# Keeping the residual stream centred through four layers, and what that moves in the scan stage

## The chip, the cores and the metric

The kernel runs on one core of a Trainium2 chip. A core has a matrix engine (TensorE, PE here), a vector engine (VectorE, DVE), a scalar engine for functions and copies (ScalarE, ACT), a general engine (GpSimd, POOL) and a queue that starts transfers (SyncE, SP); they run their own instruction streams and wait for one another by semaphores. SBUF is the on-chip memory, PSUM the memory that PE writes its sums to. The metric is the time of one execution on the device in microseconds, lower is better.

## The reference

Four layers work on x of shape (2, 2048, 128), each with a layernorm ahead of it and one behind it, and a residual add:

```python
def _layernorm(x, axis=-1, eps=1e-05):
    m = jnp.mean(x, axis=axis, keepdims=True)
    v = jnp.var(x, axis=axis, keepdims=True)
    return (x - m) / jnp.sqrt(v + eps)
...
    x = x + _layernorm(_L0_attn_ref(_layernorm(x, axis=-1), ...), axis=-1)   # time mix
    x = x + _layernorm(_L0_ffn_ref(_layernorm(x, axis=-1), ...), axis=-1)    # gated feed-forward, ternary weights
    x = x + _layernorm(_L1_attn_ref(_layernorm(x, axis=-1), ...), axis=-1)   # state-space scan
    x = x + _layernorm(_L1_ffn_ref(_layernorm(x, axis=-1), ...), axis=-1)    # mixture of 8 experts, top 2
    return x
```

The third layer, for each token t, channel (256 of them) and state n (16):

```python
        proj = x @ W_in                                  # raw, gate
        conv = conv1d(raw, conv_w, 4 taps, causal)
        h = silu(conv + conv_b)
        ts, Bmat, C = split(h @ W_x); dt = softplus(ts @ W_dt + b_dt)
        dA = exp(dt * -exp(A_log)); dBu = dt * Bmat * h
        state = dA * state + dBu;  y = sum_n state * C
        y = (y + h * D) * silu(gate);  return y @ W_out
```

## The kernel before

The residual stream X lies in SBUF with the 128 channels on the partitions and the 2 x 2048 tokens along the row, in float32. It is worked on in eight tiles (t, b) of N = 512 tokens: b is the batch, t one of four pieces of the sequence. The four layers are four phases, each with its own program on every engine and a barrier between them: the time mix (0 to about 150 us of the profile), the feed-forward (to 470 us), the scan stage (to 975 us), the experts (to the end).

A layernorm over the partitions is done so: PE multiplies X by `G.centre` (the identity less 1/128 everywhere) into PSUM, which takes the mean off; ACT squares that; PE multiplies the squares by `G.ones` (1/128 everywhere), which gives the variance on every partition; ACT makes the inverse root of it with a logarithm and an exponential; DVE multiplies the centred tile by it.

In the scan stage each engine runs `body(t, b)` once per tile. There are eight such passes, counted 0 to 7 here, each with a loop over the 16 states n. For each state, ACT makes the decays (`decay`, two instructions, dA), PE spreads one row of B over the partitions into PSUM (`spread_B`, pD), ACT puts the tile's first value into column 0 of it (`splice`, one column), DVE multiplies that by dt times u (`dBu`, in place, pD<-dtu,pD) and runs the recurrence as one scan instruction (hs), POOL multiplies the result by C (`prod`), and PE adds the products over the states. dA, hs and prod are rings of a few buffers. Work for the next tile is written between the states by hand: `prep(t, b, step)` at the states that PE_PREP, ACT_PREP and the like list, and work for the tile before it (`tail`) at others. Ahead of the change the next tile's chain is: centre matmul (PE, n=0), square (ACT, n=0), variance matmul and root (PE and ACT, n=1), the copy of the last three columns of the previous xn to the front of the buffer (the halo of the convolution) and the multiply of xn (DVE, behind scan 1), convolution (PE, n=2 to 5), silus (ACT, n=6, which need another function table than the exponentials: one table load ahead, one behind), and so on to dt at n=12 and 13 on POOL. ACT also scales and rounds one expert weight (`split_weights`) in two places per pass in some passes.

At the end of the kernel the experts' outputs come back with tokens on the partitions, are normalised there, and PE turns each group of 512 tokens back with four transposes into PSUM (R1); DVE adds that to X, and SP stores X.

## Time and profile before

| | |
|---|---|
| median of 3 runs | 1278.0 us (1276.61 to 1281.53) |
| profiled execution | 1280.58 us, span 1278.8 us |
| PE busy | 1082.7 us (85%) |
| DVE busy | 955.2 us (75%) |
| ACT busy | 748.4 us (59%) |
| POOL busy | 730.6 us (57%) |
| granted clock of PE, mean | 0.946 of full speed |

The span is the time between the first and the last instruction that the profiler saw. The shares are means over four phases with different limits; they have to be read phase by phase. A busy time counts an instruction from its start to its end, with what it stands in between.

### The profile page before, as it was taken

The numbers are of one execution on the slowest core, as the hardware profiler recorded it, in microseconds if no ns is written. First come the engines' busy times: TensorE is split into PE (matmuls) and PEld (weight loads), VectorE is DVE, ScalarE is ACT, GpSimd is POOL, SyncE is SP. The second block draws the span as 40 slices with busy tenths as digits, with TensorE's granted clock in tenths as the row PEclk, the third lists the DMA queues.
The fourth block names the chain that finished last, engine by engine and source line by source line (L and its number), as shares of the span: only waits on it lengthen the run. The fifth ranks groups of instructions, "written<-read, shape, count | busy, mean of one in ns | idle before, by whom it ended". The sixth has DMA issues, their size and how long they took to land. (4 is left out here: it accounts for less than half of the span.)

```text
span 1278.8 us, 16507 instructions
## 1 busy us (share of the span) xinstructions
PE 1082.7 (85%) x4934; PEld 547.4 (43%) x4934; DVE 955.2 (75%) x1181; ACT 748.4 (59%) x1306; POOL 730.6 (57%) x640
## 2 busy tenths in 40 slices
PE   7876799999999987888989898989898388887853
PEld 3322244444444433333334333333335277776753
DVE  4898585665755439999999999999991876565545
ACT  6586545655556255767767686857653345454445
POOL 0222261431513005899898989897983167777764
PEclk8898899999999998999999999999998589999986
DMA  7000000000000003222322222222210111111225
GB/s 232 1 0 0 1 1 1 1 1 1 1 1 1 1 0 109 100 83 93 98 84 88 86 84 92 70 69 77 73 58 9 58 36 50 51 54 51 50 58 182
DMA packets 33966, 67.21 MB, mean 53 GB/s; under 512 B 7168, under 2 KB 7360, under 8 KB 33664
## 3 DMA queue, kind: packets, MB, share of 16 engines
q1 hardware_dynamic: 28464, 55.23, 13.4%
q0 software_dynamic: 4992, 10.23, 3.0%
q8 instruction: 42, 0.69, 0.2%
q10 hardware_dynamic: 432, 0.76, 0.2%
q14 instruction: 36, 0.29, 0.1%
HBM read 56.63 MB, written 9.57 MB: 52 GB/s over the span
## 5 line engine op out<-in xcount | busy, mean ns | idle before, releaser
L1936 POOL TENSOR_TENSOR prod<-hs,csb 128x1024 f32<-128x1024 f32 x128 | 301.9, 2359 | 125.3 <-DVE hs L1982 120.0
L1982 DVE TENSOR_TENSOR_SCAN hs<-dA,first,pD 128x1024 f32<-128x1024 f32 x128 | 300.4, 2347 | 5.2 <-DVE pD L1995 0.8
L1664 PE MATMUL pY<-prod,const 128*128 128x512 f32 x512 | 241.5, 597 | 5.0 <-POOL prod L1936 5.0
L1809 ACT ACTIVATE dA<-dt,negA 128x511 f32<-128x511 f32 x256 | 169.4, 712 | 1.5 <-DVE dt L2037 1.4
L1995 DVE TENSOR_TENSOR pD<-dtu,pD 128x1024 f32<-128x1024 f32 x128 | 154.9, 1211 | 10.0 <-ACT pD L1824 9.7
L1664 PEld LDWEIGHTS pY<-prod,const 128*128 128x128 f32 x512 | 97.5, 192 | 109.9 <-issue 92.2
L2471 POOL DMA_INDIRECT g<-moe_rows,source x78 | 82.4, 1056 | 55.5 <-DVE source L2666 26.7
L2717 DVE SCALAR_TENSOR_TENSOR hid<-pR,silu 128x512 f32<-128x512 f32 x78 | 53.9, 692 | 67.2 <-ACT silu L2425 67.2
L1162 ACT ACTIVATE stage<-pR,vec 128x512 f32<-128x512 f32 x64 | 43.9, 687 | 99.7 <-PE pR L891 99.5
L2490 POOL DMA_INDIRECT moe_outs<-y,to x78 | 81.1, 1039 | 26.2 <-issue 22.8
L1824 ACT ACTIVATE pD<-first 128x1 f32<-128x1 f32 x128 | 21.6, 169 | 119.4 <-PE pD L1674 98.2
L2425 ACT ACTIVATE silu<-pR 128x512 f32<-128x512 f32 x78 | 46.6, 597 | 73.9 <-PE pR L2210 73.9
L2208 PE MATMUL pR<-x,moe_hi 128*128 128x256 f16 x312 | 85.8, 275 | 1.2 <-DVE x L2701 1.2
L2210 PE MATMUL pR<-x,moe_lo 128*128 128x256 f16 x312 | 85.7, 275 | 0.0
L2209 PE MATMUL pR<-x,moe_hi 128*128 128x256 f16 x312 | 85.7, 275 | 0.0
L576 POOL TENSOR_TENSOR o<-o,rs 128x512 f32<-128x512 f32 x8 | 14.0, 1744 | 110.0 <-DVE o L692 110.0
L1674 PE MATMUL pD<-split,sel 96*128 96x512 bf16 x128 | 50.3, 393 | 28.4 <-DVE hs L1982 28.2
L1593 PE MATMUL pQ<-xn,convw 128*128 128x512 f32 x112 | 59.3, 656 | 15.0 <-DVE xn L1966 15.0
L1200 POOL TENSOR_TENSOR K_lo<-kstage,K_hi 128x512 f16<-128x512 f32 x24 | 29.1, 1217 | 52.0 <-DVE K_hi L1267 52.0
L1206 POOL TENSOR_TENSOR A_lo<-stage,A_hi 128x512 f16<-128x512 f32 x32 | 43.0, 1348 | 27.5 <-DVE A_hi L1341 27.5
L2320 PE MATMUL pY<-moe_hi,hid_hi 128*128 x312 | 56.4, 219 | 0.8 <-DVE hid_lo L2708 0.8
L2322 PE MATMUL pY<-moe_hi,hid_lo 128*128 x312 | 56.2, 219 | 0.0
(477 smaller groups left out, 2588.1 us busy)
## 6 DMA issues: line engine op xcount, KB each, us to landing
csb<-ssm_c SPq DMA_DIRECT2D x128, 256.0 KB, 3.1
raw<-moe_w SPq DMA_DIRECT2D x12, 512.0 KB, 4.8
room<-moe_outs SPq DMA_DIRECT2D x8, 512.0 KB, 8.3
hidw<-hid_w SPq DMA_DIRECT2D x1, 2048.0 KB, 10.0
moe_rows<-xt SPq DMA_DIRECT2D x8, 256.0 KB, 2.0
outT<-X SPq DMA_DIRECT2D x8, 256.0 KB, 2.0
X<-xT SPq DMA_DIRECT2D x3, 512.0 KB, 4.1
g<-moe_rows,source POOLq DMA_INDIRECT x78, 2.6
```

Source lines behind the costliest of these rows:

```text
L1593: last = nc.tensor.matmul(Q[c][:], convw[:, c, k, :], xn[b][:, k:k + N], start=k == 0, stop=k == TAPS - 1)
L1664: last = nc.tensor.matmul(YB[c][:], G.ident, prod[:, slot(b, n), c, :], start=n == 0, stop=n == DST - 1)
L1809: last = nc.scalar.activation(dA[:, slot(b, n), c, 1:N], dt[:, b, c, 1:N], ACT.Exp, scale=negA[:, c, n:n + 1])
L1936: nc.gpsimd.tensor_tensor(prod[:, slot(b, n), :, :], hs[:, slot(b, n), :, :], csb[:, slot(b, n), :, :].to_broadcast([P, CB, N]), ALU.mult)\
L1982: nc.vector.tensor_tensor_scan(hs[:, slot(b, n), :, :].rearrange("p c n -> p (c n)"), dA[:, slot(b, n), :, :].rearrange("p c n -> p (c n)" ...
L1995: nc.vector.tensor_tensor(both_dBu(n), dtu[:, b, :, :], bcastB(n).unsqueeze(1).to_broadcast([P, CB, N]), ALU.mult)\
L2208: nc.tensor.matmul(out, w_hi, x_hi, start=start, stop=False)
L2209: nc.tensor.matmul(out, w_hi, x_lo, start=False, stop=False)
L2210: return nc.tensor.matmul(out, w_lo, x_hi, start=False, stop=stop)
L2320: nc.tensor.matmul(out, hid_hi[:, n % HR, at], w_hi, start=u == 0 and h == 0 and r == 0, stop=False)
L2471: nc.gpsimd.indirect_dma_start(g[:, i % GR, r, :], None, rows, bass.IndirectOffsetOnAxis(ap=source[:, 2 * i + r:2 * i + r + 1], axis=0))\
L2490: nc.gpsimd.indirect_dma_start(outs, bass.IndirectOffsetOnAxis(ap=to[:, 2 * i + r:2 * i + r + 1], axis=0), y[:, i % YR, r, :], None).then_ ...
```

## The change

In phase 1 ACT copies each tile's centred value from PSUM back over X (`keep_centred`), and the matmuls that read X wait for that. The output of a layernorm has mean zero over the channels, so that X stays centred from then on: the centre matmuls of the later layernorms are taken out (two late in phase 1, six at the feed-forward's second half of the head, one at its end, seven in the scan stage and six in its last pass, two at the start of the experts), and squares and multiplies read X in SBUF instead of PSUM. The result needs the mean that was taken off: x is loaded again from memory (four tiles early in the last phase, four behind the experts' outputs), and a matmul by `G.ones` into the same PSUM as the transposes adds the mean, once per group.

In the scan stage a row's square no longer waits for PE, and stands on ACT at n=15 of the pass before the one that prepares it, with the three halo columns, which DVE no longer copies. Its variance and root are at n=0. PE does the spread of state 3 ahead of the convolution. ACT does the decays of states 7 and 8 ahead of the first table load, then the splice of state 7, the silus and the second load, then the splice of state 8. The weight splits are at n=1 and 3, and POOL's dt and dtu both at n=12.

```diff
                         pe.wait_ge(S["ln1"], at(t - 1, b))
+                        pe.wait_ge(S["x_centred"], at(t - 1, b))
                     if t >= 3:
...
                     nc.scalar.activation(rstd[:, b, :], lnv[:, b, :], ACT.Exp, scale=-0.5).then_inc(S["rstd"], 1)
+
+            def keep_centred(t):
+                for b in range(B):
+                    act.wait_ge(S["ln1"], at(t, b))
+                    nc.scalar.activation(X[:, b, ds(t)], C[b][:], ACT.Copy).then_inc(S["x_centred"], 1)
 
...
 
-            def next_square(b, ready, done):
+            def next_square(b, src, ready, done):
                 act.wait_ge(ready, b + 1)
-                nc.scalar.activation(hsq[:, b, :], V[b][:], ACT.Square).then_inc(done, 1)
+                nc.scalar.activation(hsq[:, b, :], src, ACT.Square).then_inc(done, 1)
 
...
             def next_square_B(b):
-                next_square(b, S["h_centredB"], S["h_squaredB"])
+                next_square(b, X[:, b, ds(FIRST)], S["h_addedA"], S["h_squaredB"])
 
...
             inverse_roots(0)
+            keep_centred(0)
             square(1)
...
                 log_of_sums(t)
+                if t + 1 < NT:
+                    keep_centred(t + 1)
                 if 1 <= t < NT - 1:
...
                 if g == 8:
-                    centre_B(t, 0)
                     values(t, 1)
...
                     variance_A(t, 1)
-                if g == 13:
-                    centre_B(t, 1)
                 if g == 14:
...
             pe.wait_ge(S["gelu2"], NT * B * FC)
-            nc.tensor.matmul(R[0][:], G.centre, X[:, 0, 0:N], start=True, stop=True).then_inc(G.ssm["centred"], 1)
             for c in range(CB):
...
             def square_B(t, b):
-                square(b, M[b], S["squaredB"], S["centredB"], ahead(t, b))
+                square(b, X[:, b, tile(t)], S["squaredB"], S["addedA"], ahead(t, b))
 
...
             def normalise_B(t, b):
-                scale(b, M[b], S["rstdB"], S["normedB"], ahead(t, b), z[:, b, :])
+                scale(b, X[:, b, tile(t)], S["rstdB"], S["normedB"], ahead(t, b), z[:, b, :])
 
...
                         accumulate(*before(t, b), DST - LAG + n)
+                    if n == 2:
+                        spread_B(t, b, n + 1)
                     if not is_last(t, b) and n in PE_PREP:
-                        prep(*after(t, b), PE_PREP.index(n))
-                    if n + 1 < DST:
+                        prep(*after(t, b), 1 + PE_PREP.index(n))
+                    if n != 2 and n + 1 < DST:
                         spread_B(t, b, n + 1)
...
 
-            PE_PREP, PE_TAIL, SKIP_AFTER = (0, 1, 2, 3, 4, 5, 6, 8, 9, 10), (12, 14), 7
+            PE_PREP, PE_TAIL, SKIP_AFTER = (0, 2, 3, 4, 5, 6, 8, 9, 10), (12, 14), 7
 
...
                 if step == 0:
-                    act.wait_ge(S["centred"], at(t, b))
-                    nc.scalar.activation(sq[:, b, :], Q[0][:], ACT.Square).then_inc(S["squared"], 1)
+                    wait_past(act, S["scaledC"], at(t, b) - 4)
+                    wait_past(act, S["split3"], at(t, b) - B)
+                    wait_past(act, S["c_out"], 16 * (at(t, b) - B))
+                    wait_past(act, S["b_out"], 16 * (at(t, b) - B))
+                    nc.scalar.activation(sq[:, b, :], X[:, b, ds(t)], ACT.Square).then_inc(S["squared"], 1)
+                    if not is_start(t):
+                        act.wait_ge(S["conv"], chunk(t, b, CB - 1) - B * CB)
+                        nc.scalar.activation(xn[b][:, 0:TAPS - 1], xn[b][:, N:N + TAPS - 1], ACT.Copy).then_inc(S["halo"], 1)
                 elif step == 1:
...
                 elif step == 4:
+                    act.preload_act_table_set("silu_and_others")
+                    splice(*before(t, b), 7)
                     act.wait_ge(S["parked"], chunk(t, b, CB - 1))
...
                         splice(t, b, 0)
-                    if n + 1 < DST:
+                    if n == 6:
+                        decay(t, b, 7)
+                        decay(t, b, 8)
+                        if is_last(t, b):
+                            splice(t, b, 7)
+                    elif n == 7:
+                        splice(t, b, 8)
+                    elif n + 1 < DST:
                         decay(t, b, n + 1)
...
                     if not is_last(t, b) and n in ACT_PREP:
-                        prep(*after(t, b), ACT_PREP.index(n))
+                        prep(*after(t, b), 1 + ACT_PREP.index(n))
                     if is_last(t, b) and n < 2 * EARLY:
...
                         tail(*before(t, b), ACT_TAIL.index(n))
-                    if splits(t) and n in (2, 7):
-                        split_weights(t, b, (2, 7).index(n))
+                    if splits(t) and n in (1, 3):
+                        split_weights(t, b, (1, 3).index(n))
+                    if splits(t) and n == 15:
+                        prep(t + 1, b, 0)
 
...
 
-            ACT_PREP, ACT_TAIL = (0, 1, 4, 5, 6, 8, 9, 10, 11, 12), (13, 14)
+            ACT_PREP, ACT_TAIL = (0, 4, 5, 6, 8, 9, 10, 11, 12), (13, 14)
             act.preload_act_table_set("natural_log_exp_and_others")
...
                     keep(t, b, n)
-                    if not is_last(t, b) and n in (8, 11, 12, 13):
-                        prep(*after(t, b), (8, 11, 12, 13).index(n))
+                    if not is_last(t, b) and n in (8, 11, 12):
+                        prep(*after(t, b), (8, 11, 12).index(n))
+                    if not is_last(t, b) and n == 12:
+                        prep(*after(t, b), 3)
                     if is_last(t, b) and n % 2 == 0 and 0 < n <= 2 * EARLY:
...
                 if not is_start(t):
-                    nc.vector.tensor_copy(xn[b][:, 0:TAPS - 1], xn[b][:, N:N + TAPS - 1]).then_inc(S["halo"], 1)
                     dve.wait_ge(S["halo"], at(t, b) - B)
-                nc.vector.tensor_tensor(xn[b][:, TAPS - 1:], Q[0][:], rstd[:, b, :], ALU.mult)\
+                nc.vector.tensor_tensor(xn[b][:, TAPS - 1:], X[:, b, ds(t)], rstd[:, b, :], ALU.mult)\
                   .then_inc(S["normed"], 1)
...
                 sp.dma_start(by_part[:, slab(i), :], xt[:, i % 2, :, :]).then_inc(S[f"rows_in{i % 2}"], 16)
+            def rows_again(i):
+                b, t = tile_of(i)
+                sp.dma_start(again[i], G.xT[:, b, t]).then_inc(S[f"x_again{i // (GROUPS // 2)}"], 16)
+
+            for i in range(GROUPS // 2):
+                rows_again(i)
             for r in range(YR):
...
                 sp.dma_start(back[:, :, slab(i), :], by_pair[:, :, slab(i), :]).then_inc(S[f"back{i}"], 16)
+            sp.wait_ge(S["down"], UNITS)
+            for i in range(GROUPS // 2, GROUPS):
+                rows_again(i)
             for i in range(GROUPS):
...
 
+            pe.wait_ge(S["silus"], UNITS)
             for i in range(GROUPS):
-                pe.wait_ge(S["scaledC"], i + 1)
                 if i >= 2:
                     pe.wait_ge(S["addedC"], i - 1)
+                pe.wait_ge(S[f"x_again{i // (GROUPS // 2)}"], 16 * (GROUPS // 2))
+                nc.tensor.matmul(R1[:, i % 2, :], G.ones, again[i], start=True, stop=False)
+                pe.wait_ge(S["scaledC"], i + 1)
                 for j in range(TC):
                     last = nc.tensor.matmul(R1[:, i % 2, j * P:(j + 1) * P], scaled[:, i % 2, j * P:(j + 1) * P], G.ident,
-                                            start=True, stop=True)
+                                            start=False, stop=j == TC - 1)
                 last.then_inc(S["turnedC"], 1)
...
             def square(i):
-                act.wait_ge(S["centred"], late(i) + 1)
-                nc.scalar.activation(sq[:, i % 2, :], R1[:, i % 2, :], ACT.Square).then_inc(S["squared"], 1)
+                b, t = tile_of(i)
+                nc.scalar.activation(sq[:, i % 2, :], X[:, b, t], ACT.Square).then_inc(S["squared"], 1)
 
```

On ACT in the scan stage, in a pass of the loop at states 6 to 8, this stood before. dA are the decays, pD<-first a splice, h and sgate the silus; the rows begin with the decays of state 7 and end with the splice of state 8.

```order
L1809 ACTIVATE dA<-dt,negA 128x511 x2
L1823 REGISTER_ALU
L1824 ACTIVATE pD<-first 128x1
L1740 ACT_TABLE_LOAD
L1740 ACTIVATE h_1<-h_1 128x1024
L1743 ACTIVATE sgate_1<-pQ_0 128x512
L1743 ACTIVATE sgate_1<-pQ_1 128x512
L1744 ACT_TABLE_LOAD
L1809 ACTIVATE dA<-dt,negA 128x511 x2
L1823 REGISTER_ALU
L1824 ACTIVATE pD<-first 128x1
```

It now reads:

```order
L1804 ACTIVATE dA<-dt,negA 128x511 x4
L1733 ACT_TABLE_LOAD
L1818 REGISTER_ALU
L1819 ACTIVATE pD<-first 128x1
L1736 ACTIVATE h_1<-h_1 128x1024
L1739 ACTIVATE sgate_1<-pQ_0 128x512
L1739 ACTIVATE sgate_1<-pQ_1 128x512
L1740 ACT_TABLE_LOAD
L1818 REGISTER_ALU
L1819 ACTIVATE pD<-first 128x1
```

Both pairs of decays (x4) stand ahead of the first table load, the splice of state 7 between that load and the silus, and behind the second load is only the splice of state 8.

On DVE in the scan stage, in a pass of the loop around scan 1 (hs is the scan, pD<-dtu,pD the multiply ahead of the next one, sq the inverse root), this stood before:

```order
L1995 TENSOR_TENSOR pD<-dtu,pD 128x1024
L1982 SCALAR_TENSOR_TENSOR hs<-dA,first,pD 128x1024
L1964 COPY xn<-xn 128x3
L1966 TENSOR_TENSOR xn<-pQ_0,sq 128x512
L1995 TENSOR_TENSOR pD<-dtu,pD 128x1024
L1982 SCALAR_TENSOR_TENSOR hs<-dA,first,pD 128x1024
```

It now reads:

```order
L2005 TENSOR_TENSOR pD<-dtu,pD 128x1024
L1992 SCALAR_TENSOR_TENSOR hs<-dA,first,pD 128x1024
L1976 TENSOR_TENSOR xn<-X,sq 128x512
L2005 TENSOR_TENSOR pD<-dtu,pD 128x1024
L1992 SCALAR_TENSOR_TENSOR hs<-dA,first,pD 128x1024
```

The copy of three columns is gone, and the multiply that makes xn reads X instead of PSUM.

On PE in the feed-forward, where the second centre matmul of a tile's head stands among those of another tile's layers (pR and pY are sums, hidw and cv are weights), this stood before:

```order
L890 MATMUL pR_2<-hidw,hid_hi 128x512
L891 MATMUL pR_2<-hidw,hid_lo 128x512
L928 MATMUL pM_0<-X,const 128x512
L889 MATMUL pY_1<-K_hi,cv_hi 128x512
L890 MATMUL pY_1<-K_lo,cv_hi 128x512
L891 MATMUL pY_1<-K_hi,cv_lo 128x512
```

It now reads:

```order
L894 MATMUL pR_2<-hidw,hid_hi 128x512
L895 MATMUL pR_2<-hidw,hid_lo 128x512
L893 MATMUL pY_1<-K_hi,cv_hi 128x512
L894 MATMUL pY_1<-K_lo,cv_hi 128x512
L895 MATMUL pY_1<-K_hi,cv_lo 128x512
```

The matmul of X by the constant is gone, and its neighbours follow one another.

## Rows read from the trace of the kernel before

**Rows 1.** Stretches: length; busy PE, PEld, DVE, ACT, POOL; clock, DMA share, GB/s.

```profile
150.00:470.00 320.00, 312.43 (x1302) 138.17 (x1302) 191.73 (x332) 170.66 (x231) 87.32 (x68) 0.99 0.00 1
486.00:960.00 474.00, 417.99 (x977) 168.60 (x978) 458.10 (x276) 330.06 (x618) 422.06 (x349) 0.97 0.27 83
```

**Rows 2.** Timeline of DVE, first and last scan: start, duration, operation.

```profile
486.81 2.35 DVE L1982 TENSOR_TENSOR_SCAN hs<-dA,first,pD 128x1024 f32<-128x1024 f32 x1
...
956.31 2.35 DVE L1982 TENSOR_TENSOR_SCAN hs<-dA,first,pD 128x1024 f32<-128x1024 f32 x1
```

**Rows 3.** Timeline of DVE, pass 5, scans 6 to 8.

```profile
807.49 2.35 DVE L1982 TENSOR_TENSOR_SCAN hs<-dA,first,pD 128x1024 f32<-128x1024 f32 x1
...
811.00 2.35 DVE L1982 TENSOR_TENSOR_SCAN hs<-dA,first,pD 128x1024 f32<-128x1024 f32 x1
814.88 1.23 DVE L1995 TENSOR_TENSOR pD<-dtu,pD 128x1024 f32<-128x1024 f32 x1 [1.53 <-ACT pD L1824]
816.14 2.35 DVE L1982 TENSOR_TENSOR_SCAN hs<-dA,first,pD 128x1024 f32<-128x1024 f32 x1
```

**Rows 4.** Waits of DVE, 480 to 960 us: total, times, longest.

```profile
DVE pD L1995 <- ACT pD L1824: 9.7, 13, 2.4
```

**Rows 5.** Timeline of ACT, pass 5, states 7 and 8.

```profile
805.70 1.32 ACT L1809 ACTIVATE dA<-dt,negA 128x511 f32<-128x511 f32 x2
808.63 0.17 ACT L1824 ACTIVATE pD<-first 128x1 f32<-128x1 f32 x1 [1.61 <-PE pD L1674]
808.82 1.28 ACT L1740 ACT_TABLE_LOAD   x1
810.11 1.06 ACT L1740 ACTIVATE h<-h 128x1024 f32<-128x1024 f32 x1
811.08 1.07 ACT L1743 ACTIVATE sgate<-pQ 128x512 f32<-128x512 f32 x2
812.16 1.28 ACT L1744 ACT_TABLE_LOAD   x1
813.45 1.33 ACT L1809 ACTIVATE dA<-dt,negA 128x511 f32<-128x511 f32 x2
```

**Rows 6.** Waits of ACT, 486 to 960 us: total, times, longest.

```profile
ACT pD L1824 <- POOL dtu L1910: 20.4, 7, 3.9
```

**Rows 7.** Groups of DVE instructions, 480 to 960 us: busy, mean ns, idle before.

```profile
L1966 DVE TENSOR_TENSOR xn<-pQ,sq 128x512 f32<-128x512 f32 x7 | 4.8, 688 | 0.2
L1964 DVE COPY xn<-xn 128x3 f32<-128x3 f32 x6 | 4.3, 718 | 0.0
```

**Rows 8.** Timeline of POOL and DVE around pass 5's halo copy.

```profile
788.63 2.36 POOL L1936 TENSOR_TENSOR prod<-hs,csb 128x1024 f32<-128x1024 f32 x1
...
789.93 1.09 DVE L1964 COPY xn<-xn 128x3 f32<-128x3 f32 x1
```

**Rows 9.** Timeline of POOL and DVE late in phase 1.

```profile
136.58 1.26 POOL L578 TENSOR_TENSOR XA<-o,xn 128x512 f32<-128x512 f32 x1
...
136.86 1.53 DVE L729 TENSOR_TENSOR X<-X,xn 128x512 f32<-128x512 f32 x1
```

**Rows 10.** PE's centring in phase 2: line L928, and the timeline at 453.80.

```profile
L928 PE MATMUL pM<-X,const x12: 592/592/593, 205.4 to 382.0; 128*128 128x512 f32 x12
...
453.80 1.02 PE L1037 MATMUL pR<-X,const 128*128 128x512 f32 x2
454.66 1.88 PE L1040 MATMUL pR<-stage,const 128*128 128x512 f32 x4
```

**Rows 11.** Timeline of the first microseconds: ACT, PE, DVE.

```profile
11.34 1.06 ACT L440 ACTIVATE rstd<-lnv 128x1024 f32<-128x1024 f32 x1
11.75 4.16 PE L256 MATMUL pC<-X,const 128*128 128x512 f32 x4 [2.57 <-DVE G L616]
...
20.60 1.28 DVE L625 TENSOR_TENSOR_SCAN run<-pK,run,bias 128x512 f32<-128x512 f32 x1 [6.82 <-PE pK L275]
```

**Rows 12.** Busy time by engine late in the last groups, columns as in rows 1.

```profile
1268.00:1270.00 2.00, 1.90 (x9) 1.61 (x9) 0.89 (x3) 0.03 (x1) 1.87 (x5) 0.50 0.34 130
```

More of the change, by code:

```diff
@@ L42 @@
     NV += _count
-SSM_NAMES = ("logA wsum wmean wcentred carry0 centred squared variance logs rstd normed halo conv parked projected gates "
+SSM_NAMES = ("logA wsum wmean wcentred carry0 squared variance logs rstd normed halo conv parked projected gates "
          "h xproj ts_in split1 whole rest1 split2 split3 dt_in magnitude expm log1p relu "
@@ L357, in next_variance_A @@
                 next_variance(b, S["h_squaredA"], S["h_varianceA"])
-            def next_centre_B(b):
-                pe.wait_ge(S["h_addedA"], b + 1)
-                nc.tensor.matmul(V[b][:], G.centre, X[:, b, ds(FIRST)], start=True, stop=True).then_inc(S["h_centredB"], 1)
             def next_variance_B(b):
@@ L733, in next_normalise @@
                 dve.wait_ge(S["h_rstdB"], b + 1)
[L734 removed]
+                nc.vector.scalar_tensor_tensor(out=hz[:, b, :], in0=X[:, b, ds(FIRST)], scalar=WS, in1=hsq[:, b, :],
                                                op0=ALU.mult, op1=ALU.mult).then_inc(S["h_normedB"], 1)
@@ L924, in variance_A @@
                 nc.tensor.matmul(Y[b][:], G.ones, sq[:, b, :], start=True, stop=True).then_inc(S["varianceA"], 1)
-            def centre_B(t, b):
-                pe.wait_ge(S["addedA"], ahead(t, b))
-                nc.tensor.matmul(M[b][:], G.centre, X[:, b, tile(t)], start=True, stop=True).then_inc(S["centredB"], 1)
             def variance_B(t, b):
@@ L1172, in _ @@
                 square_C(NT - 1, b)
-            act.wait_ge(G.ssm["centred"], 1)
-            nc.scalar.activation(z[:, 0, :], R[0][:], ACT.Square).then_inc(G.ssm["squared"], 1)
+            act.wait_ge(S["addedC"], at(P2_ORDER.index(0), 0))
+            nc.scalar.activation(z[:, 0, :], X[:, 0, 0:N], ACT.Square).then_inc(G.ssm["squared"], 1)
             act.wait_ge(G.ssm["variance"], 1)
@@ L1578, in prep @@
             def prep(t, b, step):
-                if step == 0:
+                if step == 1:
+                    pe.wait_ge(S["squared"], at(t, b))
                     wait_past(pe, S["relu"], chunk(t, b, 0) - 1)
-                    wait_past(pe, S["scaledC"], at(t, b) - 3)
-                    nc.tensor.matmul(Q[0][:], G.centre, X[:, b, ds(t)], start=True, stop=True)\
-                      .then_inc(S["centred"], 1)
-                elif step == 1:
-                    pe.wait_ge(S["squared"], at(t, b))
                     wait_past(pe, S["logC"], at(t, b) - 3)
@@ L1625, in next_stage @@
                     else:
-                        pe.wait_ge(S["next_parked"], i)
-                        pe.wait_ge(S["next_squared"], i)
-                    nc.tensor.matmul(Q[0][:], G.centre, X[:, i % B, (i // B) * N:(i // B + 1) * N], start=True, stop=True)\
-                      .then_inc(S["next_centred"], 1)
-                else:
-                    pe.wait_ge(S["next_squared"], i + 1)
-                    if i >= 1:
                         pe.wait_ge(S["next_logs"], i)
@@ L1637, in tail @@
             def tail(t, b, step):
-                if is_final(t):
-                    pe.wait_ge((S["next_parked"], S["next_logs"])[step], EARLY)
+                if is_final(t) and step == 1:
+                    pe.wait_ge(S["next_logs"], EARLY)
                 if step == 0:
@@ L2152, in phase_moe @@
         total = hid[:, :, :].rearrange("p r (j d) -> p r j d", j=TC)
+        again_0 = sb("again4", [P, GROUPS // 2, N])
+        spent = [w[:, :, :].rearrange("p r s -> p (r s)").bitcast(F32) for w in (hid_hi, hid_lo)]
+        again = [again_0[:, i, :] for i in range(GROUPS // 2)] + [w[:, k * N:(k + 1) * N] for w in spent for k in range(2)]
         sums = sb("sums4", [P, CHUNKS])
@@ L2210, in product @@
                 return nc.tensor.matmul(out, w_lo, x_hi, start=False, stop=stop)
-            def centre(i):
-                b, t = tile_of(i)
-                nc.tensor.matmul(R1[:, i % 2, :], G.centre, X[:, b, t], start=True, stop=True).then_inc(S["centred"], 1)
             def variance(i):
@@ L2241, in turn @@
                 last.then_inc(S["turned"], 1)
-            centre(EARLY)
-            centre(EARLY + 1)
             pe.wait_ge(S["consts"], 1)
```

44 lines of the change are left out of this document (24 added, 20 removed).

## The prediction

> **What bounds the kernel now.** I read the busy time by stage first. From 150 to 470 us PE is busy 312.43 of 320 us at a clock of 0.99: whatever leaves PE there shortens the run. From 486 to 960 us DVE is busy 458.10 of 474 us, PE 417.99 and POOL 422.06 [rows 1]; this is the scan stage. Its 128 scans start between 486.81 and 956.31 us, 469.5 us for 127 periods [rows 2]. An undisturbed period is 3.51 us (807.49 to 811.00): the scan and the next state's multiply, back to back. The next one in the same place took 5.14 us, since the multiply stood 1.53 us for ACT's splice [rows 3]. 127 periods of 3.51 are 445.8 us, so 23.7 us of the stage are something else, and the question for the change is what it does to these. The waits name the largest part: DVE waited 9.7 us in 13 stalls for splices [rows 4].
>
> **The scan stage: the splice of state 8.** Before the change ACT does, at n=6, the decays of state 7 (805.70), its splice (808.63, after a wait for PE), a table load, the silu, two gate silus, a second table load, and only then, at 813.45, the decays of state 8 and their splice [rows 5]. The multiply of state 8 could have gone at 814.88 - 1.53 = 813.35. In the new order both decay pairs stand ahead. With the durations of these rows: 805.70 + 1.33 + 1.33 = 808.36; table load 1.29 (start to start) to 809.65; splice 7, 0.17, to 809.82; silu 0.97 to 810.79; both gates 1.08 to 811.87; load 1.29 to 813.16; splice 8 to 813.33. That is 0.02 us ahead of 813.35: the stall goes, but with no reserve, and splice 7, now behind a table load, leaves at 809.82 instead of 808.80, which is about when multiply 7 wants it (scan 6 began at 807.49, so its multiply begins some 2.26 us later, 809.75). Rounding the pairs down to what fits in the stream gives some 0.2 us more. I therefore leave 0.8 us over the seven passes for a splice 7 or 8 that is still late.
>
> The other stalls in the 9.7 us are of states 0, 3 and 4. They stood behind ACT's two split copies of a weight (1.04 us each, moved from n=2 and n=7 to n=1 and n=3), behind the square and root of the next row (moved), and behind PE's convolution, which waited for xn ahead of state 3's spread (reordered), and POOL's dtu (moved ahead of one product). One of the 13, 0.3 us, is before the first scan and stays. So 9.4 us of waits can go, and each costs 5.14 - 3.51 - 1.53 = 0.10 us beside the wait: 12 x 0.10 = 1.2. The term is -9.4 - 1.2 + 0.8 = **-9.8 us**; its bounds are -11 (no stall left) and -5 (half of it remains because splice 8 is late by more than the rows say).
>
> The square and halo copy that ACT now does at n=15 come ahead of state 0's decays, some 0.7 us. They cost nothing as long as ACT waits there for POOL: it waited 20.4 us in seven times for POOL's dtu at exactly that splice, mean 2.9 us [rows 6]. POOL's dtu comes one product (2.36 us) earlier after the change, which leaves about 0.5 us of that cover, and DVE reaches the splice later than ACT. Without cover it would be 0.2 to 0.7 us per pass, up to 5 us in all.
>
> **The scan stage: xn.** DVE loses six halo copies, 4.3 us (mean 718 ns, for three columns), and keeps seven multiplies of 688 ns, 4.8 us [rows 7]. The gain of 4.3 us is what I doubt most. In pass 5 the copy lasted from 789.93 to 791.02, and POOL's product, which began at 788.63, ended at 790.99 [rows 8]: the copy itself is short, and it stood there until POOL's running instruction ended. The multiply behind it read one operand from PSUM and took its normal time. After the change it reads X and the root, both in SBUF. The only two-SBUF multiply or add of this shape next to a busy POOL is in phase 1: DVE's L729 began at 136.86 and took 1.53 us, ending 0.55 us after POOL's L578, which ended at 137.84 [rows 9]. So I take it that the new multiply waits as the copy did: up to 790.99 - 789.93 = 1.06 us in five of the seven passes (the copies' mean of 0.72 against 1.09 says that not every pass waits in full). That is -4.3 + 5.3 = **+1.0 us**. Bounds: -4.3 if it doesn't wait, +3.1 if it does in all seven passes.
> The Trainium skill, GPSIMD Engine Reference, section 1 (Specifications), says that the SBUF interfaces are shared with VectorE, with contention for DVE instructions in a 2-port mode or with two SBUF inputs. It speaks against this edit: the operand moved to SBUF puts the multiply under that rule. It gives no length; if the rule did not hold here, the scan stage would gain 5.3 us more, and the sum would be that of rival B.
> The other edits here change no engine that is waited for: PE loses a centre matmul per pass and six parks leave ACT in the last pass, where DVE had no wait.
>
> **Phase 2.** Six centre matmuls go, recorded as 12 halves of 592 ns. The pace in a full stream is seen at 453.80: a matmul of this form (two halves) starts, and the next starts at 454.66, 0.86 us later [rows 10]. With PE busy 98% of the stage, 6 x 0.86 = -5.2. The seventh, at 453.80 itself, stands ahead of the spread and the variance that open the scan stage: -0.86. ACT's squares lose a wait; DVE's six normalises read two SBUF operands, but DVE (191.73 of 320) and POOL (87.32) have room [rows 1]. The term is **-6.0**, bounds -6.5 and -3.5 (if DVE's work replaces PE as the last to arrive in some of the six places).
>
> **Phase 1.** The centre matmul of the second tile started at 11.75, before ACT's last inverse root was out at 11.34 + 1.06 = 12.40. It must now wait for an ACT copy of C, about 0.55 us (half of 1.07 for two gates from PSUM [rows 5]): 12.95, later by 1.2. DVE had no work but stood 6.82 us for PE at 20.60 [rows 11], so the delay goes through. The other copies lie in ACT's idle time, and the tail loses a matmul, some -0.3. Term **+0.9**, bounds +0.3 and +1.8.
>
> **Phase 4.** A centre pair leaves the start, -0.5. At the end eight matmuls of 128x512 enter PE ahead of each group's transposes. At full clock each is 0.86 us [rows 10] and fits while PE waits for POOL. But from 1268 to 1270 us, in the last groups, PE was busy 1.90 of 2.00 us at a granted clock of 0.50, which is 1.2 GHz [rows 12]; there each costs 1.7 and there is no room. I take +0.5, bounds -0.5 and +4. The reload of x is early for half the tiles and behind the read-back of the expert outputs for the rest, needed only at the fifth group. Term **0.0**.
>
> **Sum.** -9.8 + 1.0 - 6.0 + 0.9 + 0.0 = -13.9 us. The profiled execution took 1280.6 us (span 1278.8), 2.6 above the median of 1278.0; the difference carries over to the median unchanged: 1264.1, and I give **1264 us**.
>
> **Rivals.** A difference of about 0.5% (6.4 us) is what a measurement of this kernel can tell from none.
> B: xn does not wait for POOL. Then the scan stage gains 5.3 us more: 1259 us. For it: the one wait of phase 1 is of another POOL operation. Against: it ended with POOL's instruction. Chance 0.13.
> C: the reordered ACT still delivers splice 7 or 8 late, half the waits remain (+5), and POOL's dtu no longer covers the n=15 work: 1269 to 1272. For it: 0.02 us of reserve. Chance 0.15.
> D: the change does little: phase 2 only moves its wait to DVE (-3.5), the stalls move from state 8 to state 7 (-3), and the end pays 2 us: about 1275. Chance 0.09.
> E, slower: DVE's multiply does not get in at the end of POOL's instruction, but loses to POOL's queued ones. POOL nearly always has a product ready, 2.36 us each [rows 8]. One more per pass is 7 x 2.36 = 16.5 us, which cancels the 13.9 (break-even at 2.0 us per pass); slower by 6.4 from 2.9 us per pass, so with two products: 1264 + 33 = 1297. Against: the copy and L729 both got through at the end of the first instruction [rows 8, 9]. Chance 0.04.
> My own sum, 1260 to 1267, has 0.59.
>
> **Numbers.** The range is 1256 to 1270: it takes in B, my case with its bounds and most of C, and leaves out D, E and the far end of C. Faster by over 0.5% means below 1271.6: my case, B and nearly all of C, 0.84. Same: D and the rest of C, 0.11. Slower: E and an unseen one, 0.05.
>
> **What would show it.** In the scan stage: first to last scan 460 to 462 us instead of 469.5; no wait of a multiply for ACT above 0.4 us; xn's multiplies of 1.7 us in the later passes (of 0.69: B; of 4 and more: E). Phase 2 shorter by 6 us with PE still busy 98% of it; the second tile's centre matmul at 12.95. At the end: the ones matmuls inside PE's waits, and the distance from the first transpose to the last DVE add within 1 us of before. The prediction is wrong if splice 8 is still what DVE waits for, if the end runs at 1.2 GHz with PE as its bound, or if POOL holds the multiply for more than one instruction.

## The result and the profile after

The changed kernel takes 1271.07 us (median of 9 executions, 1269.25 to 1274.82) beside 1280.66 for the kernel before on the same chip (9 executions, 1276.61 to 1281.68): a ratio of 0.9933, interval 0.9919 to 0.9948. It is faster by 9.6 us, where 13.9 were forecast. The kernel before was itself 2.7 us slower in these nine executions than the 1278.0 that the forecast stood on; the rest of the distance to 1264, 4.4 us, is a wrong sum. Taken from 1280.66, the same sum would have given 1266.8 and its upper bound 1272.7. The measured time lies among rival C's 1269 to 1272, but not for C's reasons, as the states below show.

The page of the profiled execution of the changed kernel, its span and its row of granted clock:

```profile
span 1269.3 us, 16484 instructions
...
PEclk8898899999999998999999999999896599999897
```

The span is 9.5 us shorter. The first and the last scan (DVE's timeline of the changed kernel) divide it, as [rows 2] do for before:

```profile
480.74 2.35 DVE L1992 TENSOR_TENSOR_SCAN hs<-dA,first,pD 128x1024 f32<-128x1024 f32 x1
...
945.21 2.35 DVE L1992 TENSOR_TENSOR_SCAN hs<-dA,first,pD 128x1024 f32<-128x1024 f32 x1
```

| stretch, us | before | after | difference | forecast |
|---|---|---|---|---|
| start to first scan (phases 1 and 2) | 486.8 | 480.7 | -6.1 | -5.1 |
| first to last scan | 469.5 | 464.5 | -5.0 | -8.8 |
| last scan to the end | 322.5 | 324.1 | +1.6 | 0.0 |
| span | 1278.8 | 1269.3 | -9.5 | -13.9 |

Each number is of one profile, and of the kernel before there is only one. How far such numbers move shows in the profiles of the second run and the experiments below: with the changed kernel's code, start to first scan is 479.0 to 482.1 us (eleven profiles), first to last scan 462.0 to 464.8 (five), and last scan to the end 321.6 to 328.1 (seven). So the +1.6 is not told from none, and the -5.0 could have come out as -7.5.

In the scan stage every scan start is in the trace. The start-to-start time less 3.505 us (an undisturbed period), summed over the passes by the state that the period ends in, shows where DVE loses its time. Not all of it is waiting: some 3.6 us at state 0 and 4.2 at state 2 are multiplies of DVE's own that stand there, of 128x512 and 0.60 us each (for the tile before in six passes, xn in seven). "again" is the changed kernel in a second profile (below); the lines under it are experiments. States that are not shown hold under 0.6 us together. Three more profiles, of experiments that leave the scan stage as in the changed kernel, have 5.4 to 5.5 at state 1, 7.0 to 7.1 at state 2, and 464.6 to 464.8 in all.

| us lost at state | 0 | 1 | 2 | 3, 4 | 7 | 8 | 11, 12 | first to last scan |
|---|---|---|---|---|---|---|---|---|
| before | 5.2 | 0.3 | 8.8 | 2.1 | 0.0 | 7.9 | 0.0 | 469.5 |
| after | 3.9 | 6.4 | 6.1 | 0.0 | 1.4 | 0.0 | 1.3 | 464.5 |
| again | 3.9 | 5.3 | 6.1 | 0.0 | 0.4 | 0.0 | 1.1 | 462.0 |
| dtu behind product 13 | 5.0 | 0.3 | 7.6 | 0.1 | 1.4 | 0.0 | 1.3 | 461.2 |
| spread of state 1 first | 3.9 | 0.3 | 9.1 | 0.0 | 0.0 | 0.0 | 0.9 | 459.4 |
| root in PSUM | 3.9 | 6.8 | 4.2 | 0.2 | 1.0 | 0.0 | 1.1 | 462.6 |
| both of these | 3.9 | 0.3 | 5.2 | 0.2 | 1.0 | 0.0 | 1.1 | 457.1 |
| both, and PE busy at the barrier | 3.9 | 0.3 | 4.2 | 0.0 | 0.0 | 0.0 | 0.9 | 454.5 |
| old order of states 7 and 8 | 3.9 | 4.6 | 6.7 | 0.0 | 0.0 | 8.4 | 0.0 | 468.7 |

State 8's 7.9 us are gone, and so are those of states 3 and 4. In their place stands a loss at state 1 that was 0.3 us before and that no rival named. Behind the first pass no multiply of state 0 waits for ACT, so that what ACT now does at n=15 costs nothing. DVE's waits of the changed kernel, against [rows 4] of before:

```profile
DVE pD L2005 <- ACT pD L1819: 7.3, 8, 2.7
```

Eight waits instead of 13, of 7.3 us instead of 9.7. In pass 1, DVE's timeline of the changed kernel (scan 0, the multiply and the scan of state 1):

```profile
539.09 2.35 DVE L1992 TENSOR_TENSOR_SCAN hs<-dA,first,pD 128x1024 f32<-128x1024 f32 x1
544.11 1.23 DVE L2005 TENSOR_TENSOR pD<-dtu,pD 128x1024 f32<-128x1024 f32 x1 [2.67 <-ACT pD L1819]
545.38 2.35 DVE L1992 TENSOR_TENSOR_SCAN hs<-dA,first,pD 128x1024 f32<-128x1024 f32 x1
```

The multiply waits 2.67 us for ACT's splice, which waits for PE's spread. PE's timeline of the changed kernel at the same place:

```profile
537.95 3.78 PE L1650 MATMUL pY<-prod,const 128*128 128x512 f32 x4 [2.94 <-POOL prod L1945]
541.53 1.91 PE L1579 MATMUL pQ<-sq,const 128*128 128x512 f32 x2
543.24 0.63 PE L1660 MATMUL pD<-split,sel 96*128 96x512 bf16 x1
```

PE adds up product 13 of the old tile (537.95, after standing 2.94 us for POOL), then the next row's variance (541.53), and only then spreads B for state 1 (543.24). The product was late on POOL, whose timeline in the changed kernel shows why:

```profile
529.93 2.36 POOL L1891 TENSOR_TENSOR dt<-dt,dtu 128x1024 f32<-128x1024 f32 x1
532.36 2.36 POOL L1895 TENSOR_TENSOR dtu<-dt,h 128x1024 f32<-128x1024 f32 x1
...
535.54 2.36 POOL L1945 TENSOR_TENSOR prod<-hs,csb 128x1024 f32<-128x1024 f32 x1
```

dt and dtu stand one behind the other, and product 13 begins at 535.54, behind both. Before the change it stood between them, and PE added it up without a wait ahead of state 1's spread (timelines of POOL and PE in the kernel before, same pass):

```profile
537.97 2.34 POOL L1886 TENSOR_TENSOR dt<-dt,dtu 128x1024 f32<-128x1024 f32 x1
540.27 2.34 POOL L1936 TENSOR_TENSOR prod<-hs,csb 128x1024 f32<-128x1024 f32 x1
...
542.71 2.33 POOL L1890 TENSOR_TENSOR dtu<-dt,h 128x1024 f32<-128x1024 f32 x1
```

```profile
542.83 1.88 PE L1664 MATMUL pY<-prod,const 128*128 128x512 f32 x4
544.55 1.02 PE L1582 MATMUL pQ<-X,const 128*128 128x512 f32 x2
545.96 0.39 PE L1674 MATMUL pD<-split,sel 96*128 96x512 bf16 x1 [0.39 <-DVE hs L1982]
```

In the changed kernel PE stands 2.1 to 2.9 us for product 13 in each of the seven passes that have a tile before them; in the kernel before it does in none. In pass 1 the granted clock is 0.50, or 1.2 GHz, behind that idle time, and the sum of four matmuls takes 3.78 us, twice the 1.88 that it takes elsewhere in this trace at 1.00 (busy time by engine in the changed kernel; the clock is third from the right, ahead of the share of the transfer engines and GB/s):

```profile
532.00:535.00 3.00, 3.00 (x8) 1.04 (x6) 2.96 (x3) 2.34 (x6) 2.92 (x4) 1.00 0.06 23
...
538.00:541.00 3.00, 3.00 (x4) 1.45 (x5) 2.96 (x2) 0.00 (x0) 3.00 (x4) 0.50 0.25 87
```

The multiply of xn did wait for POOL as forecast, where it got that far. The group in the changed kernel, against [rows 7], and POOL's and DVE's timelines in pass 5:

```profile
L1976 DVE TENSOR_TENSOR xn<-X,sq 128x512 f32<-128x512 f32 x7 | 6.5, 932 | 0.0
```

```profile
780.31 2.35 POOL L1945 TENSOR_TENSOR prod<-hs,csb 128x1024 f32<-128x1024 f32 x1
782.61 0.66 POOL L1938 COPY carry<-hs 128x2 f32<-128x2 f32 x1
```

```profile
781.47 1.75 DVE L1976 TENSOR_TENSOR xn<-X,sq 128x512 f32<-128x512 f32 x1
...
804.18 1.21 DVE L2005 TENSOR_TENSOR pD<-dtu,pD 128x1024 f32<-128x1024 f32 x1
```

From 781.47 the multiply stood until POOL's product ended (780.31 + 2.35 = 782.66), and took 1.75 us; POOL's small copy behind it took 0.66 instead of 0.19. But in five of the seven passes it took 0.67 to 0.7: in four of these, DVE had been held in state 1, and POOL had used that time. Rivals B and E both fall: the multiply waits, and none takes more than 1.98 us in any profile of this study.

ACT's timeline in pass 5 of the changed kernel, against [rows 5]; the multiply of state 8 is the last row above:

```profile
795.26 2.54 ACT L1804 ACTIVATE dA<-dt,negA 128x511 f32<-128x511 f32 x4
797.82 1.28 ACT L1733 ACT_TABLE_LOAD   x1
799.12 0.17 ACT L1819 ACTIVATE pD<-first 128x1 f32<-128x1 f32 x1
...
801.26 1.28 ACT L1740 ACT_TABLE_LOAD   x1
802.55 0.17 ACT L1819 ACTIVATE pD<-first 128x1 f32<-128x1 f32 x1
```

Splice 8 was out at 802.72, and DVE wanted it at 804.18: 1.5 us of reserve, not 0.02, since ACT comes to decay 7 earlier against DVE than before (3.15 us ahead of the start of scan 6, where it was 1.79).

Behind the scan stage, the first and the last matmuls of PE's scores in the changed kernel, and its busy time around them:

```profile
966.33 3.58 PE L2246 MATMUL pX<-gatew,convw 128*128 128x8 f32 x16 [4.55 <-DVE later L2541]
...
989.24 1.06 PE L2257 MATMUL pY<-ident,g 128*128 128x128 f16 x8
```

```profile
963.00:966.00 3.00, 0.00 (x0) 0.00 (x0) 1.17 (x11) 1.73 (x2) 0.53 (x4) 0.61 0.04 8
966.00:978.00 12.00, 11.67 (x52) 9.70 (x53) 2.41 (x7) 4.59 (x9) 4.54 (x4) 0.50 0.06 22
978.00:990.00 12.00, 12.00 (x81) 11.54 (x79) 4.68 (x8) 6.67 (x12) 4.57 (x4) 0.50 0.29 110
```

and the same matmuls in the kernel before:

```profile
979.00:988.00 9.00, 9.00 (x48) 7.78 (x46) 0.69 (x1) 2.48 (x5) 2.72 (x3) 0.52 0.00 0
988.00:998.00 10.00, 9.07 (x81) 8.35 (x81) 5.11 (x9) 7.28 (x14) 5.72 (x5) 0.82 0.35 134
```

PE is idle 4.55 us ahead of the scores (2.6 us before, where the pair of centre matmuls stood in between), and the clock stays at 0.50 for all of the 24 us that the scores and their transposes take. In the kernel before it is 0.52 until 988 and 0.82 in the 10 us behind. The first gather of an expert's rows starts 69.6 us behind the last scan, and 67.3 before.

### The profile page after: what moved, and what is told of

Same layout as the page of the kernel before. It is cut to its first block and busy times, and to the rows that moved or that the text cites. A ratio compares the mean times of both kernels' runs of the same rounds, so it can differ in the third digit from the quotient of the medians.

```text
span 1269.3 us, 16484 instructions
## 1 busy us (share of the span) xinstructions
PE 1080.5 (85%) x4902; PEld 548.9 (43%) x4902; DVE 953.0 (75%) x1175; ACT 749.6 (59%) x1314; POOL 735.4 (58%) x640
## 3 DMA queue, kind: packets, MB, share of 16 engines
q1 hardware_dynamic: 29616, 57.33, 13.9%
## 5 line engine op out<-in xcount | busy, mean ns | idle before, releaser
L1650 PE MATMUL pY<-prod,const 128*128 128x512 f32 x512 | 247.6, 609 | 16.9 <-POOL prod L1945 16.9
L580 POOL TENSOR_TENSOR o<-o,rs 128x512 f32<-128x512 f32 x8 | 13.9, 1743 | 110.1 <-DVE o L696 110.1
L1586 PE MATMUL pQ<-xn,convw 128*128 128x512 f32 x112 | 56.6, 641 | 3.0 <-DVE xn L1976 3.0
```

What stands on the lines that cost most here:

```text
L1650: last = nc.tensor.matmul(YB[c][:], G.ident, prod[:, slot(b, n), c, :], start=n == 0, stop=n == DST - 1)
```

## The experiments

The first four (dtu, spread, root, both) ran on one chip, and the changed kernel, as far as is known, on others. Their whole times compare with it only by way of the kernel before on each chip; the losses by state are the firmer evidence.

**dtu behind product 13 again.** Edit:

```diff
-                    if not is_last(t, b) and n in (8, 11, 12):
-                        prep(*after(t, b), (8, 11, 12).index(n))
-                    if not is_last(t, b) and n == 12:
-                        prep(*after(t, b), 3)
+                    if not is_last(t, b) and n in (8, 11, 12, 13):
+                        prep(*after(t, b), (8, 11, 12, 13).index(n))
```

> The changed kernel with one part undone: POOL makes dtu behind product 13 again, as before the change. In the changed kernel DVE lost 6.4 us in state 1 (PE spreads B for state 1 only after it stood for POOL's product 13 at state 0). Theory W: that product is late because dtu stands ahead of it on POOL; then the state-1 loss falls below 1 us, state 0 rises from 3.9 to about 5, and first to last scan falls from 464.5. Rider P: POOL is nearly full, so that DVE, no longer held in state 1, waits for POOL's port at xn instead: state 2 rises from 6.1 to about 9 us, and the stage ends near 462. Rival V: it is the variance matmul, now ahead of that spread, that makes it late; then state 1 keeps about 6 us.

Measured: 1264.36 us, ratio to before 0.9882 (0.9860 to 0.9904). State 1 loses 0.3 us instead of 6.4, state 0 5.0, state 2 7.6; the stage takes 461.2 us. DVE's waits for splices in this kernel:

```profile
DVE pD L2003 <- ACT pD L1819: 1.9, 5, 0.9
```

W holds and V falls: the variance matmul stands where it stood, and the loss is gone. P holds in part at most: state 2 is 1.5 us above the first profile of the changed kernel, but 0.5 above three others. The profiled execution was the slowest of the five, 1271.25 us: the 3.3 us that its scan stage is shorter are lost again ahead of it and behind it.

**The spread of state 1 first.** Edit:

```diff
+                    if n == 0:
+                        spread_B(t, b, n + 1)
                     if n < LAG and not is_first(t, b):
                         accumulate(*before(t, b), DST - LAG + n)
...
-                    if n != 2 and n + 1 < DST:
+                    if n not in (0, 2) and n + 1 < DST:
```

> The changed kernel, with PE's spread of B for state 1 moved ahead of the sum of the old tile's product 13 and of the variance matmul. W and V both expect the state-1 loss of 6.4 us to fall below 0.5 us. Rider P (the wait comes back at xn, for POOL's port): state 2 rises from 6.1 to about 9 us and first to last scan ends near 461; without P state 2 stays at 6 and the stage ends near 458.5.

Measured: 1265.0 us, 0.9896 (0.9866 to 0.9925). State 1 loses 0.3, state 2 9.1, the stage takes 459.4: P as expected (the stage is another 1.6 us shorter because state 7 lost nothing in this profile). The group of xn in this kernel:

```profile
L1978 DVE TENSOR_TENSOR xn<-X,sq 128x512 f32<-128x512 f32 x7 | 9.6, 1374 | 0.0
```

The mean rises from 932 to 1374 ns. What DVE no longer waits for in state 1, it waits for in part at POOL's port: 9.6 us for seven multiplies that take 4.6 undisturbed (next experiment), so 5.0 us of waits.

**The root in PSUM.** Edit, with a wait of ACT for DVE's last read of that bank:

```diff
-                nc.scalar.activation(rstd[:, b, :], lnv[:, b, :], ACT.Exp, scale=-0.5).then_inc(done, 1)
+                if done is S["rstd"]:
+                    wait_past(act, S["scaledC"], at(t, b) - 3)
+                    nc.scalar.activation(Q[0][:], lnv[:, b, :], ACT.Exp, scale=-0.5).then_inc(done, 1)
+                else:
+                    nc.scalar.activation(rstd[:, b, :], lnv[:, b, :], ACT.Exp, scale=-0.5).then_inc(done, 1)
...
-                nc.vector.tensor_tensor(xn[b][:, TAPS - 1:], X[:, b, ds(t)], rstd[:, b, :], ALU.mult)\
+                nc.vector.tensor_tensor(xn[b][:, TAPS - 1:], X[:, b, ds(t)], Q[0][:], ALU.mult)\
```

> The changed kernel, with the root that xn is multiplied by written to PSUM, so that the multiply has only one operand in SBUF. If the multiply waits for POOL's running instruction because both operands lie in SBUF: mean of xn from 932 to about 690 ns, none over 0.75 us, state 2 from 6.1 to 4.2 us, first to last scan from 464.5 to about 462.7. If it waits for anything else (its inputs, its output in SBUF): no change.

Measured: 1264.44 us, 0.9886 (0.9862 to 0.9909); state 2 at 4.2 us, the stage 462.6. The group in this kernel:

```profile
L1980 DVE TENSOR_TENSOR xn<-X,pQ 128x512 f32<-128x512 f32 x7 | 4.6, 661 | 0.0
```

With one operand in PSUM the same multiply, at the same place beside the same POOL, never waits: 0.66 us in each of the seven passes, against up to 1.78 in the profiles of the changed kernel. State 2 lost 1.9 us less, as expected. The stage's 462.6 lies within the 462.0 to 464.8 of the unchanged scan stage and does not tell by itself; the larger part of the difference in the whole execution is outside the scan stage.

**Both edits.**

> Both edits together: spread of state 1 ahead, and the root in PSUM. If the state-1 stall and the port wait are two forms of the same lateness of POOL, only the two together give the whole: state 1 under 0.5 us, state 2 at 4.2 us, first to last scan 456 to 457 us instead of 464.5, the execution about 8 us below the changed kernel. If POOL itself has become the bound of the stage, DVE waits elsewhere (for products at the scans) and the gain is 3 us or less.

Measured: first to last scan 457.1 us, state 1 at 0.3 and state 2 at 5.2 (4.2 expected). Only with both does the stage fall this far, and POOL is not its bound. But the execution took 1266.3 us, 0.9900 (0.9871 to 0.9928), no less than with one edit: in its profile the stretch behind the last scan takes 328.0 us, against 321.6 with the root in PSUM alone and the same code there.

**The changed kernel again, and the old order of states 7 and 8.** For the second, ACT's branches for n = 6 and 7 and the early table load with splice 7 are taken out again.

> The changed kernel itself once more, on the same chip as the others of this group. First to last scan 464.5 us within 0.3 (state 1: 6.4, state 2: 6.1), if these are properties of the program and not of one execution. From the last scan to the last scatter of the experts: 283.5 us if the scores' matmuls get the clock back in this execution (as in two of the four kernels with this same code behind the scan), 286.5 if they run at 1.2 GHz throughout.

> The changed kernel with ACT's order of states 7 and 8 as before the change (splice 8 behind both table loads with its decays). My step (the reorder takes the stall of state 8 away, and nothing else hangs on it): state 8 loses 7.9 us again, state 7 its 1.4 less, the stage takes 471 us. Rival: since DVE's later waits in states 1 and 2 are for a POOL that is behind, DVE held back in state 8 finds POOL further on there; these fall by some 5 us and the stage takes 466 us.

Measured: the changed kernel 1271.93 us, 0.9952 (0.9920 to 0.9984), the stage 462.0, not 464.5 within 0.3: states 1 and 7 lose 1 us less each than in the first profile, both in the first two passes. So a loss at one state differs by up to a microsecond between executions of one program; 5.3 us at state 1 are there again. The last scatter starts 288.8 us behind the last scan, later than either value expected. The old order 1277.16, 0.9969 (0.9952 to 0.9986), the stage 468.7, state 8 at 8.4. DVE's waits in it:

```profile
DVE pD L1996 <- ACT pD L1817: 11.9, 11, 1.9
```

State 8's loss comes back whole, and states 1 and 2 together lose 11.3 us where they lost 11.4 to 12.6 in the changed scan stage: that is no fall by 5 us, and the rival falls. The stage of 468.7, between the two forecasts, does not tell them apart. The reorder is worth the 8.4 us at state 8 less the 1.5 to 2.7 that it costs at states 7, 11 and 12.

**No reload, no mean at the end.**

```diff
-            for i in range(GROUPS // 2):
-                rows_again(i)
...
-            sp.wait_ge(S["down"], UNITS)
-            for i in range(GROUPS // 2, GROUPS):
-                rows_again(i)
...
-                pe.wait_ge(S[f"x_again{i // (GROUPS // 2)}"], 16 * (GROUPS // 2))
-                nc.tensor.matmul(R1[:, i % 2, :], G.ones, again[i], start=True, stop=False)
...
-                                            start=False, stop=j == TC - 1)
+                                            start=True, stop=True)
```

> The changed kernel without the reload of x and without the eight matmuls by ones; the output lacks the mean of x over the channels. From the first read of an expert row group to the last add, the changed kernel took 23.5 us and the kernel before 24.8. If the ones matmuls gained that, by keeping PE's clock up between the groups of transposes: 24.8 again, with the last groups at a clock of 0.5. If they cost time that something else saved: below 23.5. The stretch from the last scan to the last scatter should not move with the early reload if the clock alone sets it (283.5 or 286.5), and fall by some 2 us in either case if the reload's transfers are what is in the way.

Measured: 1270.93 us, 0.9933 (0.9913 to 0.9953), as the changed kernel. From the first read to the last add 24.3 us; with the mean the ten other profiles of this study have 23.5 to 25.3, so neither theory is borne out: the eight matmuls and the reload cost nothing that can be measured, and gain nothing. The scores end 42.9 us behind the last scan here too (to the start of the last one, as everywhere below), without the early reload in their way, and the last scatter is at 288.3.

**PE busy at the barrier.** Both scan edits, ten more dummy products behind the last variance matmul, and the centre pair (its result unused) put back ahead of the scores:

```diff
-                keep_busy((3, 10)[step])
+                keep_busy((3, 20)[step])
...
+            for i in range(2):
+                b, t = tile_of(EARLY + i % 2)
+                nc.tensor.matmul(R1[:, i % 2, :], G.centre, X[:, b, t], start=True, stop=True)
```

> Both edits of the scan stage (spread of state 1 ahead, root in PSUM), and PE kept busy across the barrier into the expert stage: ten more dummy products behind the last variance matmul, and two unused centre matmuls ahead of the scores. First to last scan 457 us. If the loss behind the scan comes from PE's clock falling in its idle time at the barrier: the clock stays at 1.0 or returns within 10 us, scores end at 36 to 40 us behind the last scan instead of 43, the last scatter at 280 to 284, and the execution is 1258 to 1261 us. If the clock falls anyway: as the two edits alone, 1264 to 1266.

Measured: 1258.03 us (1256.9 to 1261.17), ratio to before 0.9842 (0.9811 to 0.9872). The busy time behind the scan in this kernel:

```profile
952.00:955.00 3.00, 1.82 (x7) 0.69 (x5) 0.43 (x4) 0.95 (x1) 0.50 (x4) 1.00 0.02 5
955.00:962.00 7.00, 6.93 (x49) 5.14 (x47) 1.85 (x10) 4.22 (x8) 3.38 (x3) 0.84 0.00 1
962.00:974.00 12.00, 11.75 (x85) 10.44 (x86) 5.72 (x10) 7.29 (x14) 5.73 (x5) 0.64 0.31 121
```

The clock holds across the barrier and falls for a while later; the scores end 38.2 us behind the last scan, the first gather is at 64.9, the last scatter at 284.4. It is the fastest of all, 22.8 us below the kernel before and 13.9 below the changed kernel on the same chip. In the profiles the scan stage is 7.5 us shorter than that kernel's (454.5 and 462.0) and the stretch behind it 5.5 (320.8 and 326.3). How much of the 5.5 is the barrier's stays open, since that stretch is 321.6 us in the profile of the root in PSUM, which has no such edit.

**Which half of that matters.** The two parts apart, each on the changed kernel without the scan edits:

> The changed kernel with two unused centre matmuls put back at the start of the expert stage, where the change took them out; scan stage untouched (462 to 465 us). In seven profiles of kernels without the pair, PE idles 4.5 us there and the scores ended 40.0 (twice) or 42.4 to 42.9 us (five times) behind the last scan; with the pair, in the kernel before, PE idled 2.6 us and they ended at 40.4. If it is the removed pair that leaves PE at 1.2 GHz: scores end at 40.4 or sooner, most executions have a mean clock of 0.944 or more, and the execution is 2 to 3 us faster than the changed kernel, 1268 to 1269. If the clock comes back or not whatever stands there: 42.9 again in some executions, mean clock 0.935 to 0.941, 1271.

> The changed kernel with ten more dummy products behind the last variance matmul of the scan stage, without the pair: PE is busy to within some 2.5 us of the first score instead of 4.5. If the length of PE's idle time at the barrier is what matters: as with the pair, scores end at 40.4 us or sooner behind the last scan, 1268 to 1269 us. If it takes work at the start of the expert stage itself: 42.9, 1271.

Measured: with the pair 1268.68 us, 0.9919 (0.9888 to 0.9949), scores ended at 37.3 us; mean clocks 0.937 to 0.943. With the longer tail alone 1271.36, 0.9936 (0.9918 to 0.9955), scores at 41.6. The pair ends the scores 5 us sooner in its profile and is 2.4 to 3.3 us faster by the medians, but its interval overlaps that of the changed kernel. The profiled execution was the slowest of its four, 1272.3 us, and its stretch behind the last scan, 323.7 us, is only 0.4 shorter than the changed kernel's: the 5 us are not kept. And without the pair the clock came back in three profiles, two of them with the first gather at 66.7 us, sooner than in the kernel before. That the missing pair is why the clock stays low fits these runs, but is not settled.

## Why the prediction was wrong, point by point

**The direction and the phases ahead of the scan** were right. Phase 2 fell by 6.0 us, as forecast, from PE's first matmul there (149.77 before, 149.34 after) to the matmul of squares behind its last layer (457.23 and 450.77), not by rival D's 3.5. Phase 1 became 0.4 shorter where I had it 0.9 longer, and 0.4 are lost again between that matmul and the first scan. The second tile's centre matmul did start late, as its timeline in the changed kernel shows against [rows 11], but the delay had shrunk to 0.4 us at the first scan of keys, with PE's variance matmuls ahead of it done in 2.69 us instead of 3.14, and was gone at the tail, whose first add began at 136.86 in [rows 9]:

```profile
13.03 3.75 PE L257 MATMUL pC<-X,const 128*128 128x512 f32 x4 [3.85 <-ACT X L441]
21.01 1.28 DVE L629 TENSOR_TENSOR_SCAN run<-pK,run,bias 128x512 f32<-128x512 f32 x1 [7.23 <-PE pK L276]
...
136.93 1.53 DVE L733 TENSOR_TENSOR X<-X,xn 128x512 f32<-128x512 f32 x1
```

**The splice of state 8** was right: -7.9 us, and -2.1 at states 3 and 4, against 10.6 less 0.8. The 0.8 that I left for a late splice 7 came out as 0.4 to 1.4. I had not seen another 1.1 to 1.3 at states 11 and 12, which the old order does not have.

**The step that failed** is the sentence that lists POOL's dtu, "moved ahead of one product", among the reasons why stalls go, and with it the term of the splices: -9.8 forecast, -2.5 measured, -8.6 without state 1. The move does what I said at state 0 (-1.3 us, of which 1.1 come back when it is undone). I counted the instruction that is moved and not the one that it is moved past: product 13 comes 2.4 us later, PE takes it in order ahead of the spread of state 1, ACT's splice waits for that, and DVE for the splice. It costs 6.1 us at state 1 (5.0 in the second profile), shown by putting dtu back (0.3 us left at state 1) and by moving the spread ahead (0.3 us). Less than that is regained in the stage, 461.2 and 459.4 us where the changed scan stage has 462.0 to 464.8, since DVE then waits longer at xn or state 0.

**xn and POOL's port**: the mechanism was right, and the root in PSUM shows that it is the second SBUF operand. The Trainium skill, GPSIMD Engine Reference, section 1 (Specifications), states that rule; the trace agrees, with 1.75 us beside POOL against 0.67. It gives no length; here the wait runs to the end of POOL's instruction, which the page SBUF — State Buffer of the Trainium skill, section SBUF: two separate sides, states for that pair of ports. The size came out otherwise: I had +1.0, and state 2 lost 2.7 us less than before, because the new stall ahead of it took the wait away in up to four passes. This hid part of the error of the splices, by luck. With that stall gone (the spread of state 1 first) the waits are 5.0 us, where I had 5.3, and state 2 is at +0.3.

**Phase 4**: I had 0.0 and it was +1.6. The end cost nothing, as the run without the mean shows. The start, where I counted the removed pair as -0.5, came out at +2.3 by the first gather (69.6 and 67.3). Where the clock came back sooner without the pair, in two experiments, it is 66.7, or -0.6: so the +2.3 goes with the low clock, which I did not count. Why the clock stays low in one execution and not in another is open. The rest of the stretch varies: from the first gather to the last scatter the profiles have 217.5 to 222.3 us, and the kernel before has the lowest.

Together: 3.8 us in the scan stage and 1.6 behind it, less 1.0 better ahead of it, make the 4.4 us between -13.9 and -9.5, in these two profiles.

## What to carry to other kernels

When an instruction is moved ahead of another on a busy engine, price the one that it overtakes: who takes its result in order, and what stands behind that. Two waits in a row on one engine can be the same lateness of another engine, so that taking one away only partly counts until the other is gone too; a sum by place over all passes shows that, where the total of waits does not. Work that looks free to remove, on the engine with a variable clock and next to a barrier, may be what keeps it at speed; these runs make that a thing to look at, and do not show it.

## What was not expected of the hardware

The same program behind the scan ran its scores in 18 to 22 us, from one profile of this study to the next: they ended 40.0 us behind the last scan in two profiles, with the clock back at 1.0 some 9 us after the first score, and 42.4 to 42.9 in six (the expectation above counted five), with PE busy at 0.50 throughout in the first of the changed kernel; in its second the clock came back after 13 us. Mean clocks of whole executions differ too, 0.935 to 0.941 in 14 executions of the changed kernel, 0.940 to 0.951 in those of the kernel before, 0.944 to 0.950 with PE kept busy at the barrier, but they do not follow the scores: the profile with the pair put back has 0.938 and scores at 37.3 us, that with dtu put back 0.942 and 42.9. And a low clock reaches engines that PE only feeds: in pass 1 DVE lost 2.78 us at state 1 in the first profile of the changed kernel, where PE's sum took 3.78 us, and 1.63 in the second, where it took 2.81.
